# A decoder layer in halves: self-attention probabilities turned by DMA and mixed with the values in three f16 passes, one step later

## The reference, cut to what matters

```python
q = jnp.einsum('bse,ehd->bshd', x, wq)      # k and v likewise
qn = rms_norm(q, q_scale); kn = rms_norm(k, k_scale)
scores = jnp.einsum('bqhd,bkhd->bhqk', qn, kn)
attn = jax.nn.softmax(scores, axis=-1)
out = jnp.einsum('bhqk,bkhd->bqhd', attn, v)
return jnp.einsum('bqhd,hde->bqe', out, wo)
```

## Time and profile before

| | us |
|---|---|
| median of 3 runs | 2805.93 (2804.98 to 2810.42) |
| the profiled execution | 2802.11 |
| its span, first to last instruction | 2800.30 |
| PE busy / DVE / ACT / POOL | 2644.0 / 1679.3 / 1193.4 / 707.3 |
| mean granted TensorE clock | 0.984 |

### The profile page before, as it was taken

One profiled execution on the slowest core, in us unless ns is written; L12 is line 12 of the kernel. 1 busy time (PEld: TensorE's weight loads), 2 busy tenths in 40 slices (PEclk: granted clock), 3 DMA queues, 4 the chain that ended last, 5 costly groups with the idle time before them and its releaser, 6 DMA issues.

```text
span 2800.3 us, 46316 instructions
## 1 busy us (share of the span) xinstructions
PE 2644.0 (94%) x16726; PEld 1504.9 (54%) x16726; DVE 1679.3 (60%) x3701; ACT 1193.4 (43%) x2390; POOL 707.3 (25%) x672
## 2 busy tenths in 40 slices
PE   7999999999999999999987999998999999999988
PEld 4555555555555555555545446445445455455467
DVE  7776655655555555666657566566565565565554
ACT  4444444444444444444433542543543443443524
POOL 2222211211112111121212332422432422422413
PEclk9999999999999999999997999999999999999999
DMA  5444343444434344455421000000001001000000
GB/s 149 122 116 107 94 95 95 110 96 94 107 82 113 90 100 111 102 124 128 107 88 60 1 16 21 16 15 26 10 16 34 2 16 35 1 16 23 1 17 11
DMA packets 320477, 179.69 MB, mean 64 GB/s; under 512 B 266984, under 2 KB 269672, under 8 KB 320232
## 3 DMA queue, kind: packets, MB, share of 16 engines
q1 hardware_dynamic: 320232, 176.47, 25.1%
HBM read 78.66 MB, written 32.77 MB: 40 GB/s over the span
## 4 chain that ended last, share of the span: by engine, by line
PE 80%; DVE 12%; issue 4%; POOL 2%; ACT 2%; DMA 0%; DVEq 0%; SPq 0%; POOLq 0%; ACTq 0%
PE ps L1280 21%; PE ps L1281 20%; PE ps L1282 20%; PE ps L1356 3%; DVE mem L1114 2%; PE ps L1424 2%; POOL mem L589 2%; PE ps L1425 2%; PE ps L1426 2%; DVE mem L1118 2%; DVE mem L928 1%; PE ps L1332 1%; DVE mem L990 1%; PE ps L1434 1%; PE ps L1438 1%
## 5 line engine op out<-in xcount | busy, mean ns | idle before, releaser
L1280 PE MATMUL ps<-mem 128*128 128x512 f16 (+6 forms) x3524 | 1183.6, 344 | 37.1 <-DVE mem L990 24.1
L1281 PE MATMUL ps<-mem 128*128 128x512 f16 (+6 forms) x3524 | 1180.1, 343 | 0.0
L1282 PE MATMUL ps<-mem 128*128 128x512 f16 (+6 forms) x3524 | 1169.5, 342 | 0.0
L1280 PEld LDWEIGHTS ps<-mem 128*128 128x128 f16 (+2 forms) x3524 | 382.9, 109 | 353.6 <-issue 35.6
L1282 PEld LDWEIGHTS ps<-mem 128*128 128x128 f16 (+2 forms) x3524 | 382.0, 108 | 309.1 <-issue 5.3
L1281 PEld LDWEIGHTS ps<-mem 128*128 128x128 f16 (+2 forms) x3524 | 383.9, 109 | 290.0 <-issue 5.9
L589 POOL TENSOR_TENSOR mem<-mem 128x8 f32<-128x8 f32 x100 | 163.6, 1636 | 937.6 <-DVE mem L930 937.6
L632 POOL TENSOR_TENSOR mem<-mem 128x500 f32<-128x500 f32 (+1 forms) x231 | 268.1, 1161 | 360.3 <-ACT mem L862 207.9
L1236 DVE TENSOR_TENSOR mem<-mem 128x500 f16<-128x500 f32 (+1 forms) x231 | 144.6, 648 | 188.1 <-ACT mem L844 184.1
L990 DVE SCALAR_TENSOR_TENSOR mem<-ps,mem 128x512 f32<-128x512 f32 x100 | 69.1, 691 | 303.0 <-PE ps L1282 303.0
L646 POOL TENSOR_TENSOR mem<-mem 100x400 f32<-100x400 f32 x128 | 108.2, 856 | 332.7 <-DVE mem L1128 332.7
(11 more groups left out here) (123 smaller groups left out, 3436.1 us busy)
## 6 DMA issues: line engine op xcount, KB each, us to landing
x<-mem SPq DMA_DIRECT2D x100, 256.0 KB, 2.1
mem<-x SPq DMA_DIRECT2D x75, 256.0 KB, 2.8
mem<-in_x SPq DMA_DIRECT2D x50, 256.0 KB, 3.3
mem<-x SPq DMA_DIRECT2D x12, 1000.0 KB
out<-mem SPq DMA_DIRECT2D x6, 1000.0 KB
mem<-in_wq SPq DMA_DIRECT2D x4, 1024.0 KB, 6.3
mem<-in_wk SPq DMA_DIRECT2D x4, 1024.0 KB, 6.4
mem<-in_wv SPq DMA_DIRECT2D x4, 1024.0 KB, 5.4
```

The source lines that it names most:

```text
L1280: pe.matmul(out_ap, ah, bh, start=(i == 0), stop=False)
L1281: pe.matmul(out_ap, ah, bl, start=False, stop=False)
L1282: mm = pe.matmul(out_ap, al, bh, start=False, stop=(i == len(pairs) - 1))
```

## The change

The probabilities no longer pass through TensorE's transposes and a PSUM copy. VectorE divides the sum by 1024 before it is inverted, so that the normalised probabilities are 1024 times larger; ScalarE writes their f16 high half, GpSimd the low half, into `p_split`, padded to 128 keys with zeros set once. One DMA transpose of 112 rows of 1,024 f16 turns both halves into `pT`. VectorE makes a low half of the values. Mixing becomes 12 f16 passes, and comes one step later: on PE a step n is `scores(n + 1)`, `mix_values(n - 1)`, `project_v(n + 1)`, tiles. The output tiles move one step later as well; the factor 1024 is taken out where the output's halves are made. The bank that held the turned probabilities now holds the output tile, so that values (`ps_v`) and output tile (`ps_w`) no longer share one. `p_split` and `pT` lie where the first of two staging slots for the later weights was, so those pieces are loaded through one slot during self-attention; 13 instead of 15 are split there, and the first cross-attention group takes 7, two per sequence. The cut diff (the slots' use in the piece loads and splits, and semaphore names, are left out):

```diff
@@ -43,6 +43,8 @@
 SLOTS = 4
+P_SCALE = 1024.0
+ROWS = 112
@@ -85,7 +87,7 @@
     return [hg * TILES + t for hg in range(NHG) for t in range(TILES)
-            if hg * 32 + (t * P + P - 1) // S + 1 == n]
+            if hg * 32 + (t * P + P - 1) // S + 2 == n]
@@ -226,18 +228,21 @@
         xr = cut([3, E])
-        pT = cut([HG, S])
...
         stage_b = Cut(cut.at)([2, 2048])
+        cut = Cut(cut.at + -cut.at % 8)
+        pT = cut([2, 2 * HG, ROWS], F16)
+        p_split = cut([2, 2, HG, D], F16)
+        assert cut.at <= hb_at + 2048
+        cut = Cut(hb_at + 2048)
...
         cut = Cut(hb_at + 4096)
-        pad = -cut.at % 8
-        cut = Cut(cut.at + pad)
+        cut = Cut(cut.at + -cut.at % 8)
...
         oT_lo = cut([HG, ORING], F16)
-        v = cut([2, HG * D])
+        v = cut([2, 2, HG * D], F16)
@@ -333,8 +338,20 @@
-        B_SPLIT = [98, 100, 102, 104, 106, 108, 110, 112, 114, 116, 118, 124, 125, 126, 127]
-        B_ROWS, B_STATS, B_NORM = 110, 119, 121
+        B_SPLIT = [98, 100, 102, 104, 106, 108, 110, 112, 114, 116, 118, 124, 126]
+        B_ROWS, B_STATS, B_NORM = 111, 120, 122
+        def slot_b(n):
+            return 1 if n < len(B_SPLIT) else n % 2
+        def fills_b(n):
+            return sum(slot_b(k) == slot_b(n) for k in range(n + 1))
+        def before_b(n):
+            return max([k for k in range(n) if slot_b(k) == slot_b(n)], default=-1)
@@ -434,7 +451,7 @@
-            return range(len(B_PIECES))[B_IN_A + b:B_IN_A + b + 1]
+            return range(len(B_PIECES))[B_IN_A + 2 * b:B_IN_A + 2 * b + 2]
@@ -502,7 +519,16 @@
-            for n in range(FIRST_STEP, STEPS + 1):
+            def turn_probs(n):
+                sp.wait_ge(s["plo"], n + 1)
+                if n >= 2:
+                    sp.wait_ge(s["o"], n - 1)
+                sp.dma_start_transpose(pT[:, n % 2, :, :],
+                                       p_split[0:ROWS, n % 2, :, :, :].rearrange("p a h k -> p (a h k)")
+                                       ).then_inc(s[f"pT{n % 2}"], 16)
+            for n in range(FIRST_STEP, STEPS + 3):
@@ -529,9 +555,10 @@
                     load_keys(keys_of(0, GB), GB)
+                if 0 <= n + 1 < STEPS:
+                    turn_probs(n + 1)
...
                     turn_tile(u)
-            store_sum(ALL - 1)
@@ -596,12 +623,18 @@
+            def probs_lo(n):
+                pool.wait_ge(s["phi"], n + 1)
+                pool.tensor_tensor(p_split[0:S, n % 2, 1, :, 0:S], probs[0:S, n % 2, :, :],
+                                   p_split[0:S, n % 2, 0, :, 0:S], ALU.subtract).then_inc(s["plo"], 1)
...
+            pool.memset(p_split[:, :, :, :, :], 0.0).then_inc(s["pz"], 1)
@@ -609,6 +642,7 @@
                     norm(n + 1)
+                    probs_lo(n + 1)
@@ -727,19 +761,21 @@
+            def probs_hi(n):
+                act.wait_ge(s["norm"], n + 1)
+                if n == 0:
+                    act.wait_ge(s["pz"], 1)
+                if n >= 2:
+                    act.wait_ge(s[f"pT{n % 2}"], 16 * (n // 2))
+                act.activation(p_split[0:S, n % 2, 0, :, 0:S], probs[0:S, n % 2, :, :],
+                               ACT.Copy).then_inc(s["phi"], 1)
...
                     act.wait_ge(s["o"], n - 1)
-                act.activation(v[0:S, n % 2, :], ps_vw[0:S, :], ACT.Copy,
+                act.activation(v[0:S, n % 2, 0, :], ps_v[0:S, :], ACT.Copy,
                                scale=V_SCALE / (X_SCALE * W_SCALE)).then_inc(s["ve"], 1)
-            def take_pT(n):
-                act.wait_ge(s["pTp"], n + 1)
-                if n:
-                    act.wait_ge(s["o"], n)
-                act.activation(pT[0:S, :, :], ps_pT[0:S, 0:HG * S].rearrange(
-                    "p (h t) -> p h t", h=HG), ACT.Copy).then_inc(s["pTe"], 1)
@@ -750,21 +786,21 @@
                                         ps_o[:, 0:HG * S].rearrange("p (h t) -> p h t", h=HG)
-                                        [:, :, col:col + count], ACT.Copy)
+                                        [:, :, col:col + count], ACT.Copy, scale=1 / P_SCALE)
...
-            for n in range(FIRST_STEP, STEPS):
-                if n >= 0:
-                    take_pT(n)
+            for n in range(FIRST_STEP, STEPS + 1):
+                if 0 <= n - 1 < STEPS:
+                    take_o_hi(n - 1)
...
                     rows_hi(u)
-                if n >= 0:
-                    take_o_hi(n)
...
                     split_qk(u)
+                if 0 <= n + 1 < STEPS:
+                    probs_hi(n + 1)
@@ -960,7 +996,7 @@
                 if n >= 2:
-                    dve.wait_ge(s["pTp"], n - 1)
+                    dve.wait_ge(s["plo"], n - 1)
@@ -972,22 +1008,32 @@
                     dve.wait_ge(s["norm"], n)
-                dve.wait_ge(s["den"], n + 1)
+                dve.wait_ge(s["den"], 2 * n + 1)
+                dve.tensor_scalar(den[0:S, :], den[0:S, :], 1 / P_SCALE, None,
+                                  ALU.mult).then_inc(s["den"], 1)
+                dve.wait_ge(s["den"], 2 * n + 2)
...
                 for col, at, count in ring_runs(n * S, S, ORING):
-                    op = dve.tensor_tensor(oT_lo[:, :, at:at + count],
-                                           ps_o[:, 0:HG * S].rearrange("p (h t) -> p h t", h=HG)
-                                           [:, :, col:col + count],
-                                           oT_hi[:, :, at:at + count], ALU.subtract)
+                    op = dve.scalar_tensor_tensor(
+                        out=oT_lo[:, :, at:at + count],
+                        in0=ps_o[:, 0:HG * S].rearrange("p (h t) -> p h t", h=HG)[:, :, col:col + count],
+                        scalar=1 / P_SCALE, in1=oT_hi[:, :, at:at + count], op0=ALU.mult,
+                        op1=ALU.subtract)
                 op.then_inc(s["olo"], 1)
+            def take_v_lo(n):
+                dve.wait_ge(s["ve"], n + 1)
+                dve.scalar_tensor_tensor(out=v[0:S, n % 2, 1, :], in0=ps_v[0:S, :],
+                                         scalar=V_SCALE / (X_SCALE * W_SCALE), in1=v[0:S, n % 2, 0, :],
+                                         op0=ALU.mult, op1=ALU.subtract).then_inc(s["vlo"], 1)
...
                 dve.wait_ge(s[f"xr{w % 3}"], 16 * (w // 3 + 1))
-                dve.scalar_tensor_tensor(out=xr[:, w % 3, :], in0=ps_vw[:, :],
+                dve.scalar_tensor_tensor(out=xr[:, w % 3, :], in0=ps_w[:, :],
@@ -1027,11 +1073,13 @@
-            for n in range(FIRST_STEP, STEPS):
+            for n in range(FIRST_STEP, STEPS + 3):
...
                     subtract_max(n + 1)
+                if 0 <= n - 1 < STEPS:
+                    take_o_lo(n - 1)
@@ -1043,10 +1091,9 @@
                     inverse_sum(n + 1)
+                    take_v_lo(n + 1)
...
                     scale_q(u)
-                if n >= 0:
-                    take_o_lo(n)
@@ -1324,69 +1369,54 @@
-            def turn_probs(n):
-                pe.wait_ge(s["norm"], n + 1)
-                if n:
-                    pe.wait_ge(s["pTe"], n)
-                for h in range(HG):
-                    mm = pe.transpose(ps_pT[0:S, h * S:(h + 1) * S], probs[0:S, n % 2, h, :],
-                                      ident[0:S, 0:S])
-                mm.then_inc(s["pTp"], 1)
-            def project_v(n, added):
+            def project_v(n):
...
                 if n:
-                    pe.wait_ge(s["ve"], n)
-                if added:
-                    pe.wait_ge(s["add"], added)
-                three(ps_vw[0:S, :], [(xT_hi[:, e, b * S:(b + 1) * S], xT_lo[:, e, b * S:(b + 1) * S],
+                    pe.wait_ge(s["vlo"], n)
+                three(ps_v[0:S, :], [(xT_hi[:, e, b * S:(b + 1) * S], xT_lo[:, e, b * S:(b + 1) * S],
...
             def mix_values(n):
-                pe.wait_ge(s["pTe"], n + 1)
-                pe.wait_ge(s["ve"], n + 1)
+                pe.wait_ge(s[f"pT{n % 2}"], 16 * (n // 2 + 1))
+                pe.wait_ge(s["vlo"], n + 1)
...
                 for h in range(HG):
-                    mm = pe.matmul(ps_o[:, h * S:(h + 1) * S], v[0:S, n % 2, h * D:(h + 1) * D],
-                                   pT[0:S, h, :], start=True, stop=True)
+                    a, b = h * D, (h + 1) * D
+                    mm = three(ps_o[:, h * S:(h + 1) * S],
+                               [(v[0:S, n % 2, 0, a:b], v[0:S, n % 2, 1, a:b],
+                                 pT[0:S, n % 2, h, 0:S], pT[0:S, n % 2, HG + h, 0:S])])
...
-            def project_wo(w, taken):
+            def project_wo(w):
...
                 pe.wait_ge(s["olo"], hg * NB + (t * P + P - 1) // S + 1)
-                pe.wait_ge(s["ve"], taken)
...
                     pe.wait_ge(s["add"], w)
-                at = t * P % ORING
-                three(ps_vw[:, :], [(oT_hi[:, h, at:at + P], oT_lo[:, h, at:at + P], out_hi[:, h, :],
+                at = w * P % ORING
+                three(ps_w[:, :], [(oT_hi[:, h, at:at + P], oT_lo[:, h, at:at + P], out_hi[:, h, :],
...
```

(35 more changed lines are left out.)

## The result

The median went from 2805.45 us (2802.31 to 2810.42, 4 runs) to 2710.16 us (2708.09 to 2713.64, 4 runs): ratio 0.9661, 95% interval 0.965 to 0.9673. The forecast was 2686, its range 2664 to 2745.

The account below looks back on a forecast made before the run. It took TensorE to bound the self-attention, VectorE's and ScalarE's chain the first cross-attention group. Gains 102 + 26 + 5 less costs 5 + 2 + 2 + 4 net 120 us, giving 2686 us, range 2664 to 2745.

Parts of the forecast that it names:

- Mixing and transposes: TensorE in self-attention: transposes and f32 mixing out, f16 mixing in, saves 0.80 us a step, 102 us over 128 steps.
- Waits that go: TensorE's self-attention waits for the residual add and normalised probabilities: 26 of 34 us saved, bounds 10 and 34.
- the whole queue: SyncE's queue with 128 more DMA transposes: in time for the mixing, cost 2 us, bounds 0 and 10.
- rival 4: Mixing waits at the head of steps for late turned probabilities; some 150 us, 2836 us, slower than before; chance 0.04.
- VectorE in the first group: First group of heads: VectorE's added work fits less well at 81% busy; cost 5 us, bounds 0 and 27.
- The clock: Self-attention: TensorE's clock dips go with the long stalls, a gain of 5 us, bounds 0 and 6.
- rival 2: Self-attention: VectorE becomes the bound, through its load and contention with GpSimd; price 22 + 40 us, 2748 us; chance 0.15.
- The two pieces moved: First cross-attention group: two weight pieces more for ScalarE and VectorE cost 4 us, bounds 0 and 8.
- The start and the last steps: Zeroing at the start about 0, 2 at most; the last sequence's longer path ending self-attention costs 2 us.
- worst corner: Whole kernel, all mishaps at once: the least saving from the bounds, 67 + 10 + 0 - 27 - 14 = 36 us.
- likeliest case: Whole kernel: gains and costs come as summed, saving 85 to 135 us, 2671 to 2721 us; chance 0.75.

Follow-up runs that it names:

- e1: Against the changed kernel, SyncE issues the q/k tile's transpose ahead of the probabilities' transpose in each step; 2699.52 us, ratio 0.9625.
- e5: Against the changed kernel, the probabilities are transposed a second time into unread spare memory in steps 0 to 95; 2735.36 us, ratio 0.9753.
- e2: Against the changed kernel, ScalarE makes the weight pieces' high halves ahead of the probabilities' high half; 2704.91 us, ratio 0.9636.
- e3: Against the changed kernel, both order changes together: tile's transpose first on SyncE, weight pieces first on ScalarE; 2689.52 us, ratio 0.9582.
- e6: Against the changed kernel, VectorE's low half of the values is left out (zeros), TensorE's passes kept; 2700.60 us, ratio 0.9628.
- e9: Against the changed kernel, the two order changes on SyncE and ScalarE once more, as a repetition; 2687.82 us, ratio 0.9578, one execution of 6805 us left out.
- e7: Against the changed kernel, the first cross-attention group's seven weight pieces are spread 2, 2, 1, 1, 1 instead of 2, 2, 2, 1; 2707.56 us, ratio 0.9652.
- e8: Against the changed kernel, both order changes on SyncE and ScalarE plus the seven weight pieces spread 2, 2, 1, 1, 1; 2686.02 us, ratio 0.9568.
- e4: Against the changed kernel, the output tile goes back into the values' PSUM bank, with waits keeping both safe; 2758.46 us, ratio 0.9832.

## Why the prediction was right in direction and 24 us short

- **Mixing and transposes, 102 us: right.** Its part of 0.55 us, which I chose against 0.70, measures 0.54, and the direct count over the 128 steps gives 103.2 us. What the self-attention lost once waits (+0.3) and clock (+5.1) are taken out is 97.1 + 0.3 + 5.1 = 102.5 us.
- **Waits that go, 26 us: the step that failed.** Of the 34 us all but 2.8 did go. In the part on the queue I gave the q/k tile's transpose four steps of slack and costed the whole queue at 2 us, bounds 0 and 10. The four steps are from projection to use; SyncE gets to it only behind the probabilities' transpose. In the longest case the tile was ready at 446.63 and wanted by the scores at 453.43, 6.8 us: the 3.64 us in the queue and the landing (4.2/4.5/6.2 us for line 519, with two issues for a tile that is copied) do not fit in. It measures 17.7 us of waits and a part of the dips, and e1 and e5 show the cause from both sides. Named right was the queue, wrong what it hurts: the mixing, whose probabilities rival 4 had come late, waited for them 3.6 us in all.
- **VectorE in the first group, 5 us: too small.** I had named the waits inside its chain and not followed ScalarE, on which `probs_hi` waits for GpSimd ahead of the weight piece. I costed ScalarE at nothing because its busy time was equal; its order was not. The waits for line 974 rose from 4.3 to 17.6 us; e2 and e3 bring them to 9.6 and 11.9. The other half is VectorE's own fullness, as e6 says with 10.7.
- **The clock, a gain of 5 us: wrong in sign.** It cost 5.1. I had the dips go with the old stalls, and did not ask which new stalls would be long enough. In e3 the stretches are at 1.00 and the gain is there: 3.4 us at the lower level. (Its repetition, e9, has 10.2.)
- **Contention (rival 2): on both engines, not where I had put it.** The scaling of the sum (L1012) stayed at 0.17 us, also at 442.56 under a GpSimd operation of 1.63 us that had begun at 442.07. In the steady part it was GpSimd that stood: `probs_lo` takes 1.41 us at 446.03, beside VectorE's L991 from 445.95, and 0.95 at 119.77 without such a neighbour; its mean is 1.28 us, for which I had put 0.85. The page "SBUF — State Buffer" of the Trainium skill, section "SBUF: two separate sides", fits the row: a VectorE operation with two SBUF inputs, as L991, holds the shared pair, and the one that starts second waits. That so small an operation as the scaling goes free stands in no row of before; this one decides. VectorE stood in the first group, where its layer-norm scaling went from 0.54 to 1.17 us in 15 of 25 cases; I had looked for contention only beside the sum and the halves of q and k. At 72% VectorE is no bound in the steady part, and the price of rival 2, 22 + 40 us, did not come.
- **The two pieces moved, 4 us: right**, 5.1 measured, of which the spread wins back half.
- **The start and the last steps, 2 us**: too small to see.
- **3.5 us after the marks** belong to no step of mine. That part lasts 1265.1 us in e7, 1267.8 in e9, 1268.2 in e3 and 1270.5 in e8, all with the same code there, and 26.4, 32.2, 32.6 and 41.8 us of it are at the lower clock. So it is scatter that goes with the clock and not the change; why the clock differs there stays open.

The sum of the prediction has one slip: its worst corner, 36 us, takes 14 for all costs but VectorE's, while the bounds given for them add to 18 without the two items of 2 us. Neither the range nor the forecast rests on it. The result lies inside the likeliest case's own range, 2671 to 2721, and not by luck between errors: the large term was right, and the terms that were wrong all erred to the same side.

The theory after the result, that a cause is worth its waits plus half the time of its dips, holds between traces. By the books and by the end of the self-attention: e1 14.5 and 13.9 us faster, e2 5.1 and 4.6, e3 24.7 and 23.4, e6 12.1 and 12.4; e4 44.1 and 47.5 slower, e5 16.5 and 17.1. The medians of e1 and e3 give less, 10.6 and 20.6, about by the 3.5 us that the profile of after lies above its median. My expectation for e1, 15 to 22, was too high since I let none of its waits come back elsewhere. What part of the 11.9 us left for line 974 in e3 could still go was not tried.

## What to carry to other kernels

An engine whose busy time the change leaves equal can still cost: an operation that waits, put ahead of ones that others wait for, hands its wait on. Go through the order of each engine's program, SyncE's and ScalarE's too, and put the item with the least slack first. When a removed wait is counted as a gain, look for what is next late in the same place; here the total of waits stayed at 43 us until two reorderings brought it to 29. Count slack from when the queue reaches an instruction, not from the loop's lead.

## What the runs showed of the hardware

- A GpSimd subtraction of two SBUF operands (100x400) took 0.95 us alone and 1.41 beside a VectorE operation with two SBUF inputs; a VectorE `tensor_scalar` of 100x4 beside a GpSimd operation stayed at 0.17 us, where the one of 125x512 in the earlier trace rows took 3.39 and the one of 128x512 beside that subtraction 1.17 in place of 0.54.
- A DMA transpose of 112 rows of 1,024 f16 lands after 2.9/3.1/11.1 us (minimum, median, maximum), of 128 rows of 2,048 after 4.2/4.5/6.2, both in the changed kernel; the first occupies SyncE for 1.2 us in the median, the second for 2.1.
- f16 passes of 100 columns stand 45 to 46 ns apart whether their weights are 100 or 128 columns wide (0.55 and 0.54 us for 12).
- The granted clock fell to its lower level at some stalls of 2.2 to 4.6 us and not at others of 2.5 to 3.4; passes of 512 columns then started 0.43 us apart in place of 0.22.
